# A graph network on one core: where two of three attention layers add up their output

## What is computed

```python
def _gat_conv(x, src, dst, W, a_src, a_dst, bias, heads, ch):
    h = (x @ W).reshape(n, heads, ch)
    e = leaky_relu(alpha_src[src] + alpha_dst[dst], NEG_SLOPE)
    ex = exp(e - m[dst]);  alpha = ex / den[dst]
    out = segment_sum(h[src] * alpha[..., None], dst)
    return mean(out, axis=1) + bias
h = _gat_conv(x, src, dst, W1, as1, ad1, b1, 4, 128)
h = elu(_batch_norm(h, g1, be1))
h = _gat_conv(h, src, dst, W2, as2, ad2, b2, 4, 128)
h = elu(_batch_norm(h, g2, be2))
x = _layernorm(x + _gat_conv(h, src, dst, W3, as3, ad3, b3, 1, 64))
```

## Time and profile before

| what | before |
|---|---|
| median of 3 runs | 5185.09 us (5183.49 to 5191.42) |
| the profiled execution's own time | 5186.89 us |
| its span from first to last instruction | 5185.1 us |
| mean granted clock of TensorE | 0.912 |
| TensorE matmuls busy | 4338.7 us (84%) |
| VectorE busy | 3795.9 us (73%) |
| GpSimd busy | 2008.5 us (39%) |
| ScalarE busy | 1745.8 us (34%) |
| layers a, b, c: their blocks stored | 2130.4 to 2509.3, 2812.6 to 3304.9, 3508.7 to 3632.1 us |

### The profile page before, as it was taken

One profiled execution on the slowest core, in us unless ns is written; L12 is line 12 of the kernel. 1 busy time (PEld: TensorE's weight loads), 2 busy tenths in 40 slices (PEclk: granted clock), 3 DMA queues, 4 the chain that ended last, 5 costly groups with the idle time before them and its releaser, 6 DMA issues.

```text
span 5185.1 us, 117815 instructions
## 1 busy us (share of the span) xinstructions
PE 4338.7 (84%) x41609; PEld 3404.3 (66%) x41610; DVE 3795.9 (73%) x5814; ACT 1745.8 (34%) x3004; POOL 2008.5 (39%) x1717
## 2 busy tenths in 40 slices
PE   6999998888886977788489999579667888888886
PEld 3998888888885545344389999565444555555554
DVE  6988887877774028788466666456317999999998
ACT  0000000000000435788338777326222333333332
POOL 2888888885002017600000000000007666666663
PEclk6999999999997779999789999879668999999998
DMA  1000000000000000000000000000002111111113
GB/s 52 6 6 5 5 5 5 6 5 2 0 0 2 0 10 7 8 5 3 23 1 4 4 4 4 16 2 6 8 11 44 37 36 36 36 36 36 36 36 25
DMA packets 204304, 74.84 MB, mean 14 GB/s; under 512 B 169391, under 2 KB 189694, under 8 KB 204030
## 3 DMA queue, kind: packets, MB, share of 16 engines
q1 hardware_dynamic: 151710, 41.23, 3.6%
q0 software_dynamic: 52448, 31.60, 3.6%
HBM read 57.79 MB, written 14.88 MB: 14 GB/s over the span
## 4 chain that ended last, share of the span: by engine, by line
PE 52%; DVE 24%; issue 11%; POOL 3%; ACT 3%; DVEq 3%; DMA 2%; SPq 0%; ACTq 0%; POOLq 0%
PE ps L1201 51%; DVE adj L1159 8%; DVE scratch L861 5%; DVE adj L1151 4%; POOL by_src L512 3%; ACT scratch L651 2%; DVEq L859 1%; DVE adj L1164 1%; DVEq L338 1%; DVE scratch L1074 1%; DVE hwork L1049 0%; DMA r_dram<-adj 0%; DMA hwork<-gat_out_b 0%; DMA hwork<-gat_out_a 0%; DVE hwork L859 0%
## 5 line engine op out<-in xcount | busy, mean ns | idle before, releaser
L1201 PE MATMUL ps<-hwork,scratch 128*125 128x125 bf16 (+1 forms) x25750 | 1927.6, 236 | 102.6 <-DVE scratch L861 93.3
L1201 PEld LDWEIGHTS ps<-hwork,scratch 128*125 128x125 bf16 (+1 forms) x25750 | 1851.9, 151 | 172.1 <-DVE scratch L861 127.4
L512 POOL DMA_INDIRECT by_src<-work x782 | 1121.6, 1434 | 262.4 <-issue 224.3
L1074 DVE SCALAR_TENSOR_TENSOR scratch<-scratch,cols,adj 125x625 f32<-125x625 f32 x1125 | 939.9, 870 | 307.6 <-ACT scratch L651 289.8
L651 ACT ACTIVATE scratch<-work,cols 125x625 f32<-125x625 f32 x1125 | 965.0, 903 | 244.1 <-PE ps L1201 231.7
L541 POOL DMA_INDIRECT adj<-r_dram,adj x832 | 808.5, 972 | 493.9 <-DMA adj<-by_src 253.0
L861 DVE TENSOR_SCALAR scratch<-hwork,edge_ids 128x3125 bf16<-128x3125 uint16 x830 | 885.7, 1067 | 0.0
L1201 PEld LDWEIGHTS ps<-adj 128*125 128x125 f16 (+3 forms) x4320 | 386.4, 158 | 419.7 <-issue 381.5
L1201 PE MATMUL ps<-scratch,X 125*64 125x250 f32 (+3 forms) x3000 | 557.5, 458 | 113.2 <-DVE scratch L1074 99.8
L527 POOL IOTA adj<- 128x125 uint16 x1 | 0.2, 246 | 1635.1 <-DVEq L1123 1635.1
L1201 PE MATMUL ps<-work,adj 64*128 64x512 f32 x1664 | 470.6, 635 | 166.4 <-DVE adj L1151 122.1
(11 more groups left out here) (257 smaller groups left out, 2819.8 us busy)
## 6 DMA issues: line engine op xcount, KB each, us to landing
adj<-r_dram,adj POOLq DMA_INDIRECT x832
adj<-q_dram SPq DMA_DIRECT2D x416, 31.2 KB
by_src<-work POOLq DMA_INDIRECT x782
by_src<-adj SPq DMA_DIRECT2D x1, 4165.0 KB
adj<-by_src SPq DMA_DIRECT2D x104, 40.0 KB, 2.0
work<-in_rec SPq DMA_DIRECT2D x46, 85.0 KB, 1.9
gat_out_a<-hwork SPq DMA_DIRECT2D x5, 312.5 KB
hwork<-gat_out_a SPq DMA_DIRECT2D x1, 1562.5 KB
```

What stands on the lines that cost most here:

```text
L512: g.indirect_dma_start(by_src, bass.IndirectOffsetOnAxis(ap=pos_now[:, h, k:k + 1], axis=0), rec_in[:, h, k, :], None).then_inc(rec_sent[h ...
L1074: v.scalar_tensor_tensor(slots[:, j % SLOTS, :], slots[:, j % SLOTS, :], cols[:, 2, j, h:h + 1], adj3[:, j, ds(b * BW, BW)], ALU.add, ALU. ...
L1201: return t_.matmul(o_, l, r, start=start, stop=stop, skip_group_check=skip)
```

## The change

In layer a `add_head` now adds directly into `hid`, in layer c directly into `res`: `out_of = {"a": hid, "c": res}`, at the tile `b * BT + i`. The stores, the load back and the waits for `block_stored` and `back` are gone in these two layers. VectorE and TensorE wait for the last `scaled` instead, and so does SP before it loads gamma and beta. Line 1117 adds `X` to `res` in place. Since `hid` covers the place where the copies of W1 lay, these lie in `work` now. Layer b keeps its way through DRAM.

```diff
-        w1_whole, w1_first = hflat[0:D, 640:1152], hflat[:, 1152:1664]
-        acc_of = {"a": hflat[0:T, 0:BT * 128].rearrange("p (i c) -> p i c", i=BT), "b": acc, "c": acc}
+        w1_whole, w1_first = work[0:D, 0:512], work[:, 512:1024]
+        out_of = {"a": hid, "c": res}
...
-                    {} if n == "b" else {"aggT_ps": 0, "aggT_ready": 0, "block_ready": 0})
+                    {} if n == "b" else {"aggT_ps": 0, "aggT_ready": 0, "block_ready": 0, "block_stored": 0, "stored": 0, "back": 0})
...
-                gout = gat_out[n].rearrange("(j q) c -> q j c", q=T)
-                with sp.Fori(0, NB) as b:
-                    if n == "b":
+                if n == "b":
+                    gout = gat_out.rearrange("(j q) c -> q j c", q=T)
+                    with sp.Fori(0, NB) as b:
                         sp.wait_ge(s["block_ready"], c["block_ready"] + b + 1)
-                    else:
-                        sp.wait_ge(s["scaled"], c["scaled"] + (b + 1) * heads)
-                    sp.dma_start(gout[:, ds(b * BT, BT), :], acc_of[n][:, :, 0:fo]).then_inc(s["stored"], 16)
-                    sp.wait_ge(s["stored"], c["stored"] + 16 * (b + 1))
-                    sp.sem_inc(s["block_stored"], 1)
-                sp.wait_ge(s["stored"], c["stored"] + 16 * NB)
-                if n == "c":
-                    sp.dma_start(scratch[0:T, 0:NT * fo].rearrange("p (j c) -> p j c", j=NT), gout).then_inc(s["back"], 16)
+                        sp.dma_start(gout[:, ds(b * BT, BT), :], acc).then_inc(s["stored"], 16)
+                        sp.wait_ge(s["stored"], c["stored"] + 16 * (b + 1))
+                        sp.sem_inc(s["block_stored"], 1)
+                    sp.wait_ge(s["stored"], c["stored"] + 16 * NB)
+                    sp.dma_start(hid[:, :, 0:128], gout).then_inc(s["back"], 16)
                 else:
-                    sp.dma_start(hid[:, :, 0:128], gout).then_inc(s["back"], 16)
+                    sp.wait_ge(s["scaled"], c["scaled"] + NB * heads)
+                if n != "c":
                     for i, k in enumerate(("g", "be")):
...
-                    if h == 0:
-
-                        dve.wait_ge(s["block_stored"], c["block_stored"] + b)
                     for i in range(BT):
-                        last = v.scalar_tensor_tensor(acc_of[n][:, i, 0:fo], proj[:, i // 3, i % 3, 0:fo], small[0:T, 40 + i:41 + i],
-                                                      bias if h == 0 else acc_of[n][:, i, 0:fo], ALU.mult, ALU.add)
+                        to = out_of[n][:, ds(b * BT + i, 1), 0:fo].rearrange("p a c -> p (a c)")
+                        last = v.scalar_tensor_tensor(to, proj[:, i // 3, i % 3, 0:fo], small[0:T, 40 + i:41 + i],
+                                                      bias if h == 0 else to, ALU.mult, ALU.add)
                     last.then_inc(s["scaled"], 1)
...
-                dve.wait_ge(s["back"], c["back"] + 16)
+                if n == "b":
+                    dve.wait_ge(s["back"], c["back"] + 16)
+                else:
+                    dve.wait_ge(s["scaled"], c["scaled"] + NB * heads)
...
-            g3 = scratch[0:T, 0:NT * D].rearrange("p (j c) -> p j c", j=NT)
-            link(v.tensor_tensor(res, g3, X[:, :, 0:D], ALU.add))
+            link(v.tensor_tensor(res, res, X[:, :, 0:D], ALU.add))
```

More of the change, by code:

```diff
@@ L152, in build_gnn @@
         pos_now = sorter[:, 2 * SEND * REC:2 * SEND * (REC + 1)].rearrange("p (h k) -> p h k", h=2)
-        gat_out = {n: nc.dram_tensor(f"gat_out_{n}", (N, fo), F32, kind="Internal").ap() for n, _, _, fo in GAT}
+        gat_out = nc.dram_tensor("gat_out", (N, 128), F32, kind="Internal").ap()
         q_dram = nc.dram_tensor("q_dram", (N, D), F32, kind="Internal").ap()
@@ L1479, in _ @@
                     t, tc = bn, bn_before(li)
-                    pe.wait_ge(s["back"], c["back"] + 16)
+                    if n == "b":
+                        pe.wait_ge(s["back"], c["back"] + 16)
+                    else:
+                        pe.wait_ge(s["scaled"], c["scaled"] + NB * heads)
                     for j in range(NT):
```

## The result

| | before | after |
|---|---|---|
| median | 5185.09 us (5183.49 to 5191.42, 3 runs) | 5128.60 us (5121.89 to 5131.32, 3 runs) |
| span of the profiled execution | 5185.1 us | 5126.8 us |
| mean granted clock of TensorE | 0.912 | 0.917 |

The ratio of the runs is 0.9885, with a 95% interval of 0.9863 to 0.9908. The median fell by 56.5 us; 59.4 were forecast.

The account below looks back on a forecast made before the run. TensorE and VectorE in turn carried three quarters of the chain; idle time stood at three places. 18.6 + 23.8 + 1.5 + 16.0 - 0.5 = 59.4 us off the 5185.09 us median gave 5125.7 us, range 5114 to 5140.

Parts of the forecast that it names:

- the two large steps: Layer a: removing VectorE's standstill, 18.6 us, and the store and load at the layer's end, 23.8 us.
- The standstill: Layer a, block 1: VectorE's wait for block 0's store goes, with TensorE's slow restart; 18.6 us won, nothing late next.
- Store and load of layer a: End of layer a: TensorE's sums start just behind VectorE's last addition instead of after the load; 23.8 us won.
- The sums: End of layer a: TensorE's 50 matmuls summing over hid start at a warmer clock; 1.5 us won.
- Gamma and beta: End of layer a: their loads, issued after the last addition, stay hidden behind TensorE's sums; 0, at worst some 1 us.
- Store and load of layer c: End of layer c: line 1117 follows the last addition directly, without store and load; 16.0 us won.
- Register additions: Layer a's loop: 40 more VectorE register instructions for add_head's addresses, mostly overlapped; 0.5 us lost.
- One sign that the prediction named for being wrong: Layer a: passes longer than 23.4 us where TensorE's clock is at 1.00.
- A: Layer a: TensorE's clock falls otherwise, two dips more or fewer, 5 to 8 us either way; chance 0.20.
- B: Layer a, block 1: the standstill moves to another wait on SP or GpSimd, giving 5144 us; chance 0.07.
- C: Layer a's add_head: dynamic addressing on VectorE makes it slower, 5205 us at 2 us per register instruction; chance 0.02.
- D: Whole change: it doesn't take hold, something still waits for a load back, 5185 us; chance 0.01.

Follow-up runs that it names:

- a place for each block: Kernel before, with layer a adding up each block in its own place in hwork, no wait for block_stored there, stores and load kept: 5167.89 us, ratio 0.9963.
- the records later: SENT_FIRST 17 instead of 18, moving one turn of the records' loop into layer a: kernel before 5228.19 us, changed kernel 5127.77 us.

## Why the prediction was right

The time lay in the range, 2.9 us above the forecast, and the two large steps and layer c's were right in mechanism and in size. That the total came so close is partly luck, as shown below the steps. By the prediction's own steps:

1. *The standstill*, 18.6 us: the interval fell by 41.96 - 23.35 = 18.6. Nothing was late next, shown by the run with a place for each block and by the later records. GpSimd ended 4 us later, at about 2183, as worked out.
2. *Store and load of layer a*, 23.8 us: 25.52 us from the last reciprocal to TensorE's sums became 1.80, so 23.7. The fit of the Trainium skill, page "DMA: Bandwidth & Descriptors", section "Anatomy of one DMA — SWDGE (gpsimd) path", would have given an estimated 8.4 us here; the 23.7 us in the trace, and 22.7 us of span in the run with this end alone, speak against using it for SP's DMAs.
3. *The sums*, 1.5 us: this term was too high. The first sums did fall from 8.60 to 7.38 us, but the second sums, over the squares, rose from 7.38 to 8.75. In these stretches of the changed kernel each of the two starts at the lower level, or falls to it, and ends at the upper one:

```profile
2488.00:2491.00 3.00, 2.63 (x15) 2.66 (x16) 0.23 (x1) 0.00 (x0) 0.00 (x0) 0.67 0.13 38
2492.00:2495.00 3.00, 3.00 (x27) 3.00 (x27) 0.00 (x0) 0.00 (x0) 0.00 (x0) 0.92 0.00 0
2503.00:2507.00 4.00, 3.71 (x17) 3.71 (x18) 0.23 (x1) 0.00 (x0) 0.00 (x0) 0.50 0.02 4
2509.00:2512.00 3.00, 3.00 (x25) 2.85 (x24) 0.00 (x0) 0.00 (x0) 0.00 (x0) 0.91 0.00 0
```

   But the profile of before is the odd one here. Three other kernels keep this load (a place for each block, layer c alone, the records later). Theirs took 7.65 to 7.89 us for the first sums and 8.56 to 8.69 for the second. And the kernel with layer b's load hidden, which has the change in layer a, took 7.38 and only 7.12. The rows of the kernel with the records later, and of this one:

```profile
2575.92 7.65 PE L1201 MATMUL ps<-hwork,ones 125*125 125x128 f32 x50 [25.72 <-DMA hwork<-gat_out_a]
2591.11 8.56 PE L1201 MATMUL ps<-scratch,ones 125*125 125x128 f32 x50 [7.54 <-DVE scratch L1101]
```

```profile
2487.62 7.38 PE L1203 MATMUL ps<-hwork,ones 125*125 125x128 f32 x50 [1.84 <-DVE hwork L1047]
2502.54 7.12 PE L1203 MATMUL ps<-scratch,ones 125*125 125x128 f32 x50 [7.54 <-DVE scratch L1104]
```

   So what the change itself won at the sums was 0.3 to 0.5 us, and the long second sums aren't its price. From layer a's last reciprocal to layer b's first it was 197.4 us before, 196.1 to 196.3 in the three, and 172.2 in the changed kernel.
4. *Gamma and beta*, 0: hidden, and VectorE's line behind the sums was released by TensorE. The cover held with the sums at 7.38 us.
5. *Store and load of layer c*, 16.0 us: 16.0, and in the separate run too.
6. *Register additions*, 0.5 us: too low. Line 1045 by itself shows the register work and the idle time it left:

```profile
L1045 DVEq FUSED_REGOPS  x40: 69/69/94, 2100.4 to 2421.4; - x40
its engine sat idle before it (us, times) until:
  DVE small L1040: 1.4, 8
```

   Only the first of five is seen, 0.17 us ahead of each of the eight `add_head`, 1.4 us in all; the other four are hidden, as argued from line 908. In the intervals it comes to 0.13 + 0.05 us a block, 0.7 us in all. What the sum lacks beside it is the 0.7 us more at each of three branches back, 2.0 us, which no step had.

One sign that the prediction named for being wrong did show, by a little: four passes of layer a took 23.5 us at a granted clock of 1.00, where it wanted at most 23.4. The kernel before has them at 23.4, so the 0.13 us are the register work. That limit was too tight, for the kernel before itself has a pass of 23.75 us at 1.00. VectorE's line behind the sums, 1096 in the prediction, is 1097.

Of the rivals, A took part, and to both sides. Two early passes of layer a took 24.4 and 26.0 us where they had 23.3 and 23.75, which cost 3.4 us. Three losses behind the standstill, of 2.2 to 2.9 us, didn't come, which won 7.4. Net this is 4.0 us of the 20.0 that layer a won, and no step had forecast it. Layer b gave 2.9 back: 1.9 in one pass with a branch back (34.95 us at a clock of 0.95, against 32.92 at 1.00), the rest at its end. Here the profile of before was the lucky one: the kernel before with the records later, which has the same code there, took 798.1 us in this stretch, the changed kernel 798.5. So a gain and a loss that no step had nearly cancelled; without the one or the other the total would have been 3 to 4 us away, with the same mechanism. B, C and D fell.

## What to carry to other kernels

A wait of one engine for "stored" can be a wait for whatever stands ahead of the store in the queue that issues it, here the sending of records by a third engine. So look at every place where an edit removes a wait, not only at the transfer's own time, and move a known amount of the suspected work past it: where the time follows, that was the cause. A place for each block cost only the register work, where the next step's tile had room for it, and where it has none, the load back can follow the reader tile by tile.

## What was not expected of the hardware

TensorE's granted clock fell to the lower level in passes of layer a that do the same work as their neighbours, without a long idle time ahead of the fall (1.1 us in the stretches above). A pass of 23.3 us at a mean clock of 1.00 took 24.4 to 24.9 us at 0.93, and 25.5 to 26.0 at 0.87. With layer a written out this came once in each of blocks 1 to 4 (25.6 to 25.8 us), and in two of the first four intervals (24.6 and 24.7 us). The two later kernels with the same written-out layer had other falls, six of the small and two of the large kind, at the same passes in both, and the layer took the same 450.9 us.

And a branch back in a loop of four passes left VectorE with nothing to do for 4.3 to 4.7 us in layer a, over all traces, but cost only some 2 us a pass in layer b, where TensorE's clock mostly stayed at 1.00.
